# First pass: ScalarE takes its second exponent ahead of the norms, and the feed-forward runs one step later

## The reference: what is computed

```
x = x + tanh(g_xattn[0]) * attention(layernorm(x), ctx, ctx)           # 16 heads, no weights, no mask
x = x + tanh(g_ffn[0])   * (fp8(layernorm(x)/s_in) @ fp8(W/s_k)) * s_in*s_k + bias
x = x + tanh(g_xattn[1]) * attention(layernorm(x)Wq, ctx Wk, ctx Wv, mask) Wo + bo
x = x + tanh(g_ffn[1])   * fake_quant(layernorm(x)*gamma + beta) @ ternary(W).T
```

## Time and profile before

| | us |
|---|---|
| timed runs: median of 3 (lowest to highest) | 2249.64 (2249.06 to 2306.87) |
| the profiled execution: its own time | 2246.3 |
| its span, first to last instruction | 2244.5 |
| PE busy | 1947.8 (87%) |
| DVE busy | 1941.7 (87%) |
| ACT busy | 1637.9 (73%) |
| POOL busy | 1122.4 (50%) |
| DVE, maxima (line 844), both passes, 512 instructions | 624.8, 1220 ns each |
| ACT, exponents of the first pass (line 573), 256 instructions | 261.8, 1023 ns each, 81.2 idle before them |

### The profile page before, as it was taken

How to read it: one execution, slowest core, us unless ns; L and a number is a source line. 1 busy time by engine, 2 the same in 40 slices (tenths; PEclk the granted TensorE clock), 3 DMA queues, 4 the chain that set the end, 5 groups by cost and what they waited for, 6 DMA issues and landing times. The chain is left out here.

```text
span 2244.5 us, 73785 instructions
## 1 busy us (share of the span) xinstructions
PE 1947.8 (87%) x24736; PEld 1429.4 (64%) x24736; DVE 1941.7 (87%) x3958; ACT 1637.9 (73%) x2631; POOL 1122.4 (50%) x1905
## 2 busy tenths in 40 slices
PE   3888888888888886799999999999999999999857
PEld 2665665665665654577777777777777777777545
DVE  4788888888888886589999999999999999999579
ACT  1777777777777776377777777777777777777579
POOL 2566666666666664234444444444444444444310
PEclk8999999999999998799999999999999999999879
DMA  2221211211211110100000000000000000000035
GB/s 79 65 63 59 62 60 59 63 60 59 63 60 59 61 53 13 30 23 24 21 21 21 21 21 21 21 21 21 21 21 21 22 23 21 21 21 18 1 111 189
DMA packets 113869, 95.23 MB, mean 42 GB/s; under 512 B 13440, under 2 KB 113792, under 8 KB 113792
## 3 DMA queue, kind: packets, MB, share of 16 engines
q1 hardware_dynamic: 113792, 94.23, 13.4%
HBM read 60.63 MB, written 33.55 MB: 42 GB/s over the span
## 5 line engine op out<-in xcount | busy, mean ns | idle before, releaser
L844 DVE TENSOR_REDUCE a_nmax<-bank_max 128x8 f32<-128x1024 f32 x512 | 624.8, 1220 | 132.9 <-DVEq L843 127.1
L1113 PE MATMUL bank_max<-UM,U 32*128 32x256 f32 x4096 | 585.7, 403 | 13.7 <-PEq L1226 7.1
L1120 PE MATMUL bank_exp<-UM,U 32*128 32x256 f32 x4096 | 556.7, 389 | 3.9 <-PEq L1261 3.9
L1135 PE MATMUL bank_o<-probs,V 128*17 128x128 f32 x8192 | 325.9, 276 | 170.4 <-PEq L1131 166.3
L641 ACT ACTIVATE probs<-bank_exp 128x1024 f32<-128x1024 f32 x256 | 262.2, 1024 | 272.3 <-ACTq L640 272.3
L1113 PEld LDWEIGHTS bank_max<-UM,U 32*128 32x128 f32 x4096 | 353.1, 185 | 105.6 <-issue 99.6
L1135 PEld LDWEIGHTS bank_o<-probs,V 128*17 128x17 f32 x8192 | 192.0, 96 | 326.2 <-issue 325.4
L530 POOL TENSOR_SCALAR UM<-U,heads_eo 128x512 f32<-128x512 f32 x128 | 88.6, 692 | 605.7 <-POOLq L528 605.7
L1120 PEld LDWEIGHTS bank_exp<-UM,U 32*128 32x128 f32 x4096 | 372.6, 185 | 5.8 <-issue 5.2
L941 DVE CAST bank_max<-ff_qT 128x1024 f32<-128x1024 bf16 x256 | 314.4, 1228 | 8.9
L573 ACT ACTIVATE probs<-bank_exp 128x1024 f32<-128x1024 f32 x256 | 261.8, 1023 | 81.2 <-ACTq L572 81.2
(11 more groups left out here) (168 smaller groups left out, 4252.0 us busy)
## 6 DMA issues: line engine op xcount, KB each, us to landing
X<-in_x SPq DMA_DIRECT2D x128, 128.0 KB, 2.1
ctx<-in_ctx SPq DMA_DIRECT2D x128, 128.0 KB, 2.0
out_y<-U SPq DMA_DIRECT2D x128, 128.0 KB, 1.7
ctx<-out_y SPq DMA_DIRECT2D x128, 128.0 KB, 2.0
out_y<-X SPq DMA_DIRECT2D x64, 256.0 KB, 2.1
ff_qq<-in_mask_BxSxS_ik SPq DMA_DIRECT2D x128, 64.0 KB, 1.8
X<-in_L_xattn_Wq SPq DMA_DIRECT2D x1, 256.0 KB, 2.8
X<-in_L_xattn_Wk SPq DMA_DIRECT2D x1, 256.0 KB, 3.1
```

What stands on the lines that cost most here:

```text
L844: return v.tensor_reduce(a_nmax[:, k2, n * H // 2:(n + 1) * H // 2], max_pair[:, :, :, :].rearrange("p i h t -> p (i h) t"), axis=AX.X, op ...
L1113: last = mm(max_pair[:, r % 2, 2 * c:2 * c + 2, :], U[now][32 * r:32 * r + 32, c, :], UM[now][32 * r:32 * r + 32, DC + c, :, :], start=not ...
L1120: last = mm(exp_pair[:, r % 2, 2 * c:2 * c + 2, :], U[before][32 * r:32 * r + 32, DC + c, :], UM[before][32 * r:32 * r + 32, c, :, :], sta ...
L1135: last = mm(bank_o[32 * j:32 * j + VW, (2 * c + n) * P:(2 * c + n + 1) * P], V[k4][:, 8 * c + 2 * r + e, :], a_probs[n][:, r % 2 * HG + 2 ...
```

## The change

Nothing that is computed changes, nor any buffer. What changes is the order on each engine, and the step in which the feed-forward's parts run. The names that follow have the line numbers of the kernel before, and those in the rows of the changed kernel are a few higher.

ScalarE: in every step the second exponent (`exp_pair_of(0)`) now follows the copies out of PSUM. Of the four norms of a pair of steps, one (`ff_xy`, first block) runs behind the second exponent of the odd step, one (`ff_xy`, second block) at the head of the even step, one (`xn0`) behind the second exponent of the even step, and one (`xn1`) at the head of the odd step. The copy of the product (`ff_y`) moves from odd to even steps, and the copy `ff_qT` from even to odd.

```diff
@@ -213,6 +213,7 @@
         y_used = sem("y_used")
         fq_used = sem("fq_used")
         fx_made = sem("fx_made")
+        ff_read = sem("ff_read")
         m_made = sem("m_made")
         y_out = sem("y_out")
         attn_x = sem("attn_x")
@@ -486,7 +487,7 @@
                         pool.sem_inc(slot_used, 1)
                     else:
                         v_ins.then_inc(v_made, 1)
-                if odd and live(-5):
+                if not odd and live(-6):
 
                     pool.wait_ge(grid_made, 1)
                     pool.sem_inc(grid_made, -1)
@@ -579,6 +580,10 @@
 
             def step_a(i, k, live):
                 odd = k % 2 == 1
+                if odd and live(2):
+                    normed(a_xn[1], i + 2, (k // 2 + 1) % 2, 3).then_inc(xn_made, 1)
+                if not odd and live(-5):
+                    normed(ff_xy[:, 1, :], i - 5, (k + 7) // 2 % 2, 1).then_inc(fx_made, 1)
                 if live(-2):
                     exp_pair_of(1)
                 if live(1):
@@ -594,26 +599,27 @@
                     act.wait_ge(shift_Td, 1)
                     act.sem_inc(shift_Td, -1)
                     nc.scalar.activation(sh_T[(k + 1) % 2], bank_tb[1][:, 0:4 * P], ACT.Copy).then_inc(shift_out, 1)
-                if odd and live(-7):
-                    if live(-11):
+                if not odd and live(-8):
+                    if live(-12):
                         act.wait_ge(y_used, 1)
                         act.sem_inc(y_used, -1)
                     act.wait_ge(fy_made, 1)
                     act.sem_inc(fy_made, -1)
-                    nc.scalar.activation(a_y[(k - 7) // 2 % 2].rearrange("p b n -> p (b n)"), bank_m[:, :], ACT.Copy,
+                    nc.scalar.activation(a_y[k // 2 % 2].rearrange("p b n -> p (b n)"), bank_m[:, :], ACT.Copy,
                                          scale=scales[:, 3:4]).then_inc(y_out, 1)
+                if live(-2):
+                    exp_pair_of(0)
                 if odd and (live(3) or live(-5)):
                     act.wait_ge(norm_made, 1)
                     act.sem_inc(norm_made, -1)
                 if odd and live(-5):
+                    if live(-7):
+                        act.wait_ge(ff_read, 1)
+                        act.sem_inc(ff_read, -1)
                     normed(ff_xy[:, 0, :], i - 5, k // 2 % 2, 0)
-                    normed(ff_xy[:, 1, :], i - 4, k // 2 % 2, 1).then_inc(fx_made, 1)
                 if not odd and live(2):
-                    for n in range(2):
-                        normed(a_xn[n], i + 2 + n, (k // 2 + 1) % 2, 2 + n).then_inc(xn_made, 1)
-                if live(-2):
-                    exp_pair_of(0)
-                if not odd and live(-6):
+                    normed(a_xn[0], i + 2, (k // 2 + 1) % 2, 2).then_inc(xn_made, 1)
+                if odd and live(-7):
                     act.wait_ge(fq_T, 1)
                     act.sem_inc(fq_T, -1)
                     act.sem_inc(fq_used, 1)
@@ -875,11 +881,11 @@
                     mine(v.drain())
                     settle()
                     vec.sem_inc(attn_x, 1)
-                if not odd and live(-6):
+                if odd and live(-7):
 
                     vec.wait_ge(grid_added, 1)
                     vec.sem_inc(grid_added, -1)
-                    if live(-8):
+                    if live(-9):
                         vec.wait_ge(fq_used, 1)
                         vec.sem_inc(fq_used, -1)
                     v.tensor_tensor(ff_qq[:, :, :].rearrange("p b n -> p (b n)"), a_t, a_e, ALU.subtract)\
@@ -890,7 +896,7 @@
                     vec.sem_inc(max_read, 1)
                     n_hi = mine(v.tensor_copy(sh_v[:, :, :, 0], a_nmax[:, k % 2, :].rearrange("p (i b) -> p i b", i=4)))
                 y = a_y[k // 2 % 2]
-                if not odd and live(-8):
+                if odd and live(-9):
 
                     vec.wait_ge(y_out, 1)
                     vec.sem_inc(y_out, -1)
@@ -900,10 +906,10 @@
                     vec.wait_ge(x_added, 1)
                     vec.sem_inc(x_added, -1)
                     n_bn = mine(v.bn_stats(st6f[:, :], xs(i - 3)))
-                if not odd and live(-8):
+                if odd and live(-9):
                     settle(n_y)
-                    v.scalar_tensor_tensor(xs2(i - 8), y.rearrange("p b n -> p (b n)"), gate[:, 2:3],
-                                           xs2(i - 8), ALU.mult, ALU.add).then_inc(y_used, 1)
+                    v.scalar_tensor_tensor(xs2(i - 9), y.rearrange("p b n -> p (b n)"), gate[:, 2:3],
+                                           xs2(i - 9), ALU.mult, ALU.add).then_inc(y_used, 1)
                 if live(0):
                     settle(n_hi)
                     v.tensor_tensor(sh_v[:, :, :, 1], a_nmax[:, k % 2, :].rearrange("p (i b) -> p i b", i=4),
@@ -918,13 +924,15 @@
                 elif not odd and live(5):
                     settle()
                     vec.sem_inc(stats_made, 1)
-                if odd and live(-5):
+                if not odd and live(-6):
 
                     vec.wait_ge(fx_made, 1)
                     vec.sem_inc(fx_made, -1)
                     mine(v.tensor_scalar(a_t, ff_xy[:, :, :].rearrange("p b n -> p (b n)"), scales[:, 2:3], None,
                                          ALU.mult))
                     settle()
+                    if live(-4):
+                        vec.sem_inc(ff_read, 1)
                     mine(v.tensor_scalar(a_e.bitcast(U32), a_t.bitcast(U32), EXPONENT, None, ALU.bitwise_and))
                     settle()
                     v.tensor_scalar(a_e, a_e, F8_LEAST, F8_ROUND, ALU.max, ALU.mult).then_inc(grid_made, 1)
```

## The result

| | before | after |
|---|---|---|
| timed runs of one comparison: median (lowest to highest) | 2252.97 (2249.06 to 2306.87) | 2376.64 (2346.47 to 2380.58) |
| ratio | | 1.0532, 95% interval 1.0441 to 1.0623 |
| span of the profiled execution | 2244.5 | 2377.9 |
| first pass, to VectorE's first seed of `bank_max` (CAST) | 914.3 | 983.5 |
| second pass, first to last such CAST | 1183.1 | 1246.7 |

The changed kernel is 5.3% slower; I had forecast 2273, no measurable change. Of the 133.4 us between the spans, 69.2 arise in the first pass, where I expected 24, and 63.6 in the second, of which the change touches no line.

What follows compares the result with a forecast made beforehand. The prediction took VectorE to bound even steps and GpSimd's queue odd ones: 6.19+7.07 = 13.26 a pair instead of 12.91, +21 us, and +3 for turns, so 2270 profiled and 2273 as median, range 2252 to 2300.

Steps and rivals of the forecast that it cites:

- Second and third pass: 0: Passes behind the edited first one: claimed that the change adds no time there.
- Rival 2: First pass, odd step: `ff_qq` starts just before GpSimd's power, which waits for it; 0.6 more a pair, 2309 us; chance 8%.
- The skill's lock: Port pair shared by VectorE and GpSimd: exclusive for a whole instruction; the forecast went by a trace row against it.
- GpSimd's queue in the odd step: First pass: norm factors, masks and addition to `X` queue behind the rounding's addition, delaying VectorE's statistics to G+5.76.
- G+7.07: First pass, odd step: next first maximum 7.07 us after G, the end of the even step's third rounding instruction.
- The even step: First pass, VectorE: from first maximum to the end of the third rounding instruction 6.19 us.
- The turn: First pass's 13 loop turns: VectorE reaches the branch without slack, 0.2 us more each, +3 us.

Runs made afterwards that it cites:

- the changed kernel with the short loop: Changed kernel with the second pass's hardware loop written as 4 steps a turn instead of 8; measured 2317.2, ratio 1.0129 against the kernel before.
- the power unheld: Changed kernel, 4-step second-pass loop, plus two small waited-for VectorE fills ahead of `ff_qq` in each odd step of the first pass; measured 2286.2.

## Why the prediction was wrong

- **"Second and third pass: 0" failed**, and it is the larger part: 63.6 of the 110 us between 2270 and the profiled 2380. I had taken code that is not edited for code whose time doesn't change. The view that would have warned me is TensorE's own: a loop of 1826 instructions (that many stand in the trace from one branch to the next), and one of three timed runs at 2306.87, 57 above the other two, which I had read as noise. The first pass's loop of 1450 was not fetched anew in any trace. The Trainium skill, Runtime: NRT & Kernel Launch, section "Instruction fetch mechanics", gives TensorE room for 2048 instructions in blocks of 256, first in, first out. As an estimate from this page the loop is 7.1 blocks and fits if it touches no ninth, and the trace before agrees (6 packets in 1030 us). It also calls the crossing between blocks mostly hidden; the trace after agrees for the crossings within a turn (under 0.1 us together). The same section says that a taken branch whose target isn't in the current window of two pages must wait for a fetch: the 3.4 to 5.0 us of the changed kernel agree with such a wait, but the branches of 0.2 us before don't agree with a window of two.
- **Without the second pass the forecast still fails**: the changed kernel with the short loop takes 2317, above the range of 2252 to 2300. The step that failed there is the power's wait in the odd step.
- **Rival 2 happened**, to which I gave 8%. Odd step 7.55, by its working 7.65; its 2309 for the 2317 of the short-loop kernel. I had named what decides it (0.1 us, which of the two starts first) and then trusted, which show a VectorE instruction starting inside a running power. They can't speak of the other order. The hold of 0.47 a pair is worth 28 to 31 us. The skill's lock, named in the prediction, holds in one direction here: a power behind a started `ff_qq` waits (1.49), an `ff_qq` behind a started power doesn't (0.66 to 0.69).
- **GpSimd's queue in the odd step: right.** The term was G+7.07. With the power unheld the odd step measures 7.08. Its parts: GpSimd without a pause, idle time ahead of the statistics (1.50, 0.83 with the power unheld), both gaps ahead of the maxima gone. That it fits to 0.01 is luck: from the addition to the statistics it is 0.25, I had 0.15, and from the statistics to the next maximum 1.18, I had 1.31.
- **The even step: right in kind**, 6.28 for 6.19, 5 us over 60 pairs. One piece I had put at nothing: where VectorE now signals `ff_read`, behind the first rounding instruction, the second starts 0.63 behind it (414.77 to 415.40) and not 0.52 (405.00 to 405.52 before).
- **The turn: mis-sized.** 0.2 more was 0.6 more (0.80 for 0.18), and the even step behind it 0.13 longer: 13 times 0.75 is 10 us where I had 3. I took the middle between two rows that both came from a VectorE with slack.
- **The sum by what was measured:** 60 pairs of +0.92 are 55, 13 turns 10, and the 4 that are left of the 69.2 stand in the two ends of the pass and in the even steps with a fallen clock; the second pass 63.6; together 133.

The likeliest case failed by two events of small cause: 0.05 us on which of two engines starts first, and something that tips the fetching of a long loop. What tips it stays open; the runs show that 96 instructions ahead of the loop do.

## What to carry to other kernels

Moving work between steps of a software pipeline puts it into another place of *each* engine's queue; write out the slowest follower's whole queue behind it, here GpSimd's, and put what is ready early (the norm factors) ahead of what is ready late (the rounding). Where two engines share a path and the order of two starts is open by 0.1 us, give both orders a large chance. Before predicting "0" for untouched code, look at the length of its loop on the engine with the most instructions and at outliers among the runs of before: here a loop of 1826 instructions was a cliff, one of 1450 was not, and half the length cost nothing.

## What the runs showed of the hardware

- A TensorE loop of 1826 instructions either runs without fetches (branch 0.2 us, 6 packets of 16 KB in 14 turns) or is fetched whole in each turn (3.4 to 5.0 us, some 9 packets a turn). With 96 instructions added between the passes all turns are of the second kind, with 256 added 7 of 13. With half the loop there is nothing of it (28 branches, longest 0.22). What tips it, also within one kernel (its runs at 2249 and 2307), stays open.
- Behind each of the 13 standstills of 3.4 to 5.0 us of the changed kernel TensorE's granted clock fell to half for 3.4 or 6.8 us; with 256 added it did so behind 6 of 7, and the turn without the fall was 1.8 to 2.9 us shorter. A fall of 3.4 us in the first pass lengthened a pair of steps by 1.35.
- GpSimd's power of 1.02 us and a VectorE subtraction of 0.66 overlap freely if the power starts first (by 0.30 and 0.48 in two kernels), and the power is stretched to 1.24, 1.49 or 1.54 if the subtraction does, by how much of it is left.
- A loop turn cost 0.80 in VectorE's step, and 0.13 in the next, behind a step that ends in the statistics' aggregate. Behind one that ends in the rounding, whose last instruction isn't counted among those VectorE waits for at the turn, VectorE came 0.33 late and the next step was as much shorter. That this wait is the difference is argued, not tried.
